# Causal attention in a two-layer decoder: keys turned one group after the queries, a new order of the prologue, and the output weights split inside the first groups

## The reference, cut to what matters

```python
qkv = jnp.einsum('bsd,de->bse', x, Wqkv)                 # 512 x 1536
q, k, v = jnp.split(qkv, 3, axis=-1)
q = _layernorm_scale_only(q, q_ln_scale)                 # over all 512 columns
k = _layernorm_scale_only(k, k_ln_scale)
scores = jnp.einsum('bshd,bthd->bhst', q / jnp.sqrt(32), k)   # 16 heads of 32
scores = jnp.where(causal, NEG_INF, scores)
attn = jax.nn.softmax(scores, axis=-1)
ctx = jnp.einsum('bhst,bthd->bshd', attn, v)
out = jnp.einsum('bsd,de->bse', ctx.reshape(B, S, D_MODEL), out_W)
```

## Time and profile before

| | |
|---|---|
| time, median of 3 runs | 2142.49 us (2141.91 to 2142.78) |
| profiled execution, its time | 2137.15 us |
| its span, first to last instruction | 2135.3 us |
| PE busy in the span | 1864.2 us (87%) |
| DVE, ACT, POOL busy | 1249.0, 920.2, 288.9 us |
| mean granted TensorE clock | 0.946 of 2.4 GHz |

### The profile page before, as it was taken

The page is one execution under the profiler, slowest core; times in us unless marked ns, Lnnn a source line. Parts: engine busy times, 40 slices in busy tenths (PEclk is TensorE's granted clock), DMA queues, the critical chain, the costliest instruction groups (busy, mean ns, idle before and its releaser), DMA issues. The chain is left out here.

```text
span 2135.3 us, 33023 instructions
## 1 busy us (share of the span) xinstructions
PE 1864.2 (87%) x12272; PEld 1514.4 (71%) x12272; DVE 1249.0 (58%) x2330; ACT 920.2 (43%) x2376; POOL 288.9 (14%) x347
## 2 busy tenths in 40 slices
PE   6979999999966899999999967888887488889966
PEld 5869999998954788888888855666665355555543
DVE  3445444444425665654565335677776378878847
ACT  2234333333323433333332224555556388888821
POOL 0000000000001111211111001223333221111001
PEclk9989999999988899999999988899998799999988
DMA  3122000000122221111110121000001377465234
GB/s 101 51 89 70 21 21 21 21 21 21 35 60 79 84 65 40 45 35 31 40 40 16 40 80 40 11 31 31 31 20 41 112 194 173 125 159 138 80 112 138
DMA packets 86253, 136.62 MB, mean 64 GB/s; under 512 B 9480, under 2 KB 25480, under 8 KB 86096
## 3 DMA queue, kind: packets, MB, share of 16 engines
q1 hardware_dynamic: 86096, 134.52, 21.8%
HBM read 79.88 MB, written 21.05 MB: 47 GB/s over the span
## 5 line engine op out<-in xcount | busy, mean ns | idle before, releaser
L1941 ACT ACTIVATE e_p<-e_s_ps,e_nb 128x512 f32<-128x512 f32 x256 | 174.8, 696 | 50.7 <-DVE e_nb L1989 49.2
L1164 PE MATMUL yp<-ccy,toep 128*128 128x288 f32 x640 | 178.7, 429 | 19.7 <-POOL ccy L892 13.6
L1433 ACT ACTIVATE p<-p,nb,rq 128x128 f32<-128x128 f32 (+1 forms) x256 | 136.8, 540 | 121.0 <-DVE nb L1524 121.0
L1989 DVE TENSOR_REDUCE e_nb<-e_s_ps 128x2 f32<-128x1024 f32 x128 | 155.7, 1217 | 50.9 <-PE e_s_ps L2066 50.9
L2076 PE MATMUL e_t_ps<-ident,e_p 128*128 128x128 f32 x1024 | 145.8, 281 | 23.8 <-DVE e_pT L1996 12.8
L1164 PEld LDWEIGHTS yp<-ccy,toep 128*128 128x128 f32 x640 | 124.0, 202 | 54.5 <-POOL ccy L892 14.8
L2076 PEld LDWEIGHTS e_t_ps<-ident,e_p 128*128 128x128 f32 x1024 | 117.9, 144 | 60.3 <-issue 50.3
L80 PE MATMUL q_ps<-a_xt_hi,wq_hi 128*128 128x256 f32 x512 | 151.9, 297 | 4.1 <-DVE wo_lo L112 4.1
L1062 DVE SCALAR_TENSOR_TENSOR hm<-gu_ps,us_col,sg 128x256 f32<-128x256 f32 x88 | 42.3, 481 | 182.0 <-ACT sg L971 182.0
L82 PE MATMUL q_ps<-a_xt_hi,wq_lo 128*128 128x256 f32 x512 | 146.6, 286 | 0.0
L81 PE MATMUL q_ps<-a_xt_lo,wq_hi 128*128 128x256 f32 x512 | 146.5, 286 | 0.0
(11 more groups left out here) (277 smaller groups left out, 5167.5 us busy)
## 6 DMA issues: line engine op xcount, KB each, us to landing
x_after<-n_r SPq DMA_DIRECT2D x24, 512.0 KB, 3.0
toep<-padded_kernels SPq DMA_DIRECT2D x32, 256.0 KB, 3.4
qs<-e_xh SPq DMA_DIRECT2D x64, 128.0 KB, 2.6
qs<-e_xl SPq DMA_DIRECT2D x64, 128.0 KB, 2.6
ks<-e_ch SPq DMA_DIRECT2D x64, 128.0 KB, 2.6
ks<-e_cl SPq DMA_DIRECT2D x64, 128.0 KB, 2.6
x<-x_after SPq DMA_DIRECT2D x12, 512.0 KB, 4.6
x<-in_x SPq DMA_DIRECT2D x8, 512.0 KB, 4.0
```

The lines of the kernel that those rows point to most:

```text
L1164: last = pe.matmul(yp[:, lo % 2, 0:NCOL], toep[h % 2][:, (lo - li) * P:(lo - li + 1) * P], ccy[h % 2][:, li, 0:NCOL], start=(li == 0), sto ...
L1433: act.activation(p[n % 3][:, h, part[t]], p[n % 3][:, h, part[t]], ACT.Exp, bias=nb[i][:, t, h:h + 1], scale=rq[u][:, t:t + 1], accum_out= ...
L1941: act.activation(pr[i][:, a, :], s_ps[i][:, a, :], ACT.Exp, bias=nb[i][:, a:a + 1], accum_out=sums[t][:, j, q:q + 1]).then_inc(e_done, 1)
L1989: dve.tensor_reduce(nb[i][:], s_ps[i][:], AX.X, ALU.max, negate=True).then_inc(nb_done, 1)
```

## The change

The computation and the number of instructions of each kind stay as they are. Four things move.

In the steps, turn_k and turned_k of tile t of the next batch go from g = t + 1 to g = t + 2, so keys of tile 0 are turned at g = 2 and those of tile 1 at g = 3; turn_q, turned_q and ACT's keys stay at g = t + 1. For batch 0 alone the units run q0, q1, k0, k1, v0, v1, with tile t in bank t (unit_bank, unit_place and unit_count keep the counts right), and queries and keys are turned into spare banks 0 and 1 by tile. In the prologue the pieces of Wq are split ahead of x, the six pieces of Wq, Wk and Wv alone are split there, and x of batch 1 is turned ahead of the value units. The two pieces of out_W are split at the end of steps 1 and 2.

```diff
-        q_bank, k_bank = spare[2], spare[3]
+        q_bank = lambda b, t: spare[2 if b else t]
+        k_bank = lambda b, t: spare[3 if b else t]
...
-        def unit_count(b, t):
+        def unit_count(b, i, t):
-            return t + 1 if b == 0 else 4 + t if b == 1 else 4 * b + t - 1
+            return i + 1 if b == 0 else 4 + t if b == 1 else 4 * b + t - 1
+        def unit_bank(b, i, t):
+            return t if b == 0 or i == 2 else i
+        def unit_place(b, i, t):
+            return 6 * b + (T * i + t if b == 0 or i == 2 else 2 * t + i)
...
# POOL, rstds
-                    pool.wait_ge(mv_done, 2 * n + 2)
+                    pool.wait_ge(mv_done, 2 * n + 2 if b else 3 + t)
...
# ACT, prologue
+                split.round_hi(act, 0, 2)
                 for r in range(2):
                     round_x(0, r)
-                split.round_hi(act, 0, len(split.pieces))
+                split.round_hi(act, 2, 6)
+                for t in range(T):
+                    turned_q(0, t)
+                for r in range(2):
+                    round_x(1, r)
                 for t in range(T):
                     keys(0, t)
-                    turned_q(0, t)
                 for t in range(T):
                     values(0, t)
-                for r in range(2):
-                    round_x(1, r)
# ACT, end of a step
+                    if n in (1, 2):
+                        split.round_hi(act, 5 + n, 6 + n)
...
# DVE, prologue
+                split.take_lo(dve, 0, 2)
                 for r in range(2):
                     lo_x(0, r)
-                split.take_lo(dve, 0, 4)
+                split.take_lo(dve, 2, 4)
                 dve.wait_ge(rows_loaded, 32)
-                for i in range(2):
-                    centre(0, 0, i)
-                split.take_lo(dve, 4, len(split.pieces))
-                for i in range(2):
-                    centre(0, 1, i)
+                for t in range(T):
+                    centre(0, t, 0)
+                split.take_lo(dve, 4, 6)
+                for t in range(T):
+                    centre(0, t, 1)
+                for r in range(2):
+                    lo_x(1, r)
                 dve.wait_ge(set_up, 3)
                 for t in range(T):
                     turned_k(0, t)
-                for r in range(2):
-                    lo_x(1, r)
# DVE, in a step and at its end
-                    if g in (1, 2) and b + 1 < B:
-                        turned_k(b + 1, g - 1)
+                    if g in (2, 3) and b + 1 < B:
+                        turned_k(b + 1, g - 2)
+                    if n in (1, 2):
+                        split.take_lo(dve, 5 + n, 6 + n)
...
# PE, prologue
-                for unit in range(6):
-                    pe.wait_ge(split.lo_done, (2, 4, 4, 4, 6, 6)[unit])
+                for unit in range(4):
+                    if unit % 2 == 0:
+                        pe.wait_ge(split.lo_done, unit + 2)
                     project(0, unit)
                 for t in range(T):
                     turn_q(0, t)
-                    turn_k(0, t)
                 for r in range(2):
                     turn_x(1, r)
+                pe.wait_ge(split.lo_done, 6)
+                for unit in (4, 5):
+                    project(0, unit)
+                for t in range(T):
+                    turn_k(0, t)
# PE, in a step
                     if g in (1, 2) and b + 1 < B:
                         turn_q(b + 1, g - 1, n + 1)
-                        turn_k(b + 1, g - 1, n + 1)
+                    if g in (2, 3) and b + 1 < B:
+                        turn_k(b + 1, g - 2, n + 1)
```

More of the change, by code:

```diff
@@ L1415, in keys @@
                     act.wait_ge(rstd_done, n + 1)
-                    act.wait_ge(p_free[1], unit_count(b, t))
+                    act.wait_ge(p_free[unit_bank(b, 1, t)], unit_count(b, 1, t))
                     act.activation(kn[t][:], kn[t][:], ACT.Copy, scale=rstd[:, t, 1:2]).then_inc(kn_done, 1)
@@ L1420, in turned_q @@
                     act.wait_ge(q_turned, T * b + t + 1)
-                    act.activation(qT[b % 2][:, :, t, :], q_bank, ACT.Copy).then_inc(q_copied, 1)
+                    act.activation(qT[b % 2][:, :, t, :], q_bank(b, t), ACT.Copy).then_inc(q_copied, 1)
                 def values(b, t):
@@ L1492, in centre @@
                     n, out, row = T * b + t, (qn, kn)[i][t], (qs_row, ks_row)[i]
-                    dve.wait_ge(p_mm, 6 * b + 2 * t + i + 1)
-                    dve.bn_stats(st[:, t, i, :], p_ps[i][:]).then_inc(st_done, 1)
+                    place, bank = unit_place(b, i, t), unit_bank(b, i, t)
+                    centred = 4 * b + place - 6 * b
+                    dve.wait_ge(p_mm, place + 1)
+                    dve.bn_stats(st[:, t, i, :], p_ps[bank][:]).then_inc(st_done, 1)
                     if b:
                         dve.wait_ge(ve_done, n - 1)
-                    dve.wait_ge(st_done, 2 * n + i + 1)
+                    dve.wait_ge(st_done, centred + 1)
                     dve.bn_aggr(mv[:, t, i, :], st[:, t, i, :]).then_inc(mv_done, 1)
-                    dve.wait_ge(mv_done, 2 * n + i + 1)
+                    dve.wait_ge(mv_done, centred + 1)
                     if b:
                         dve.wait_ge((q_turned, k_turned)[i], n - 1)
-                    dve.scalar_tensor_tensor(out[:], p_ps[i][:], mv[:, t, i, 0:1], row[:], ALU.subtract, ALU.mult)\
-                       .then_inc(p_free[i], 1)
+                    dve.scalar_tensor_tensor(out[:], p_ps[bank][:], mv[:, t, i, 0:1], row[:], ALU.subtract, ALU.mult)\
+                       .then_inc(p_free[bank], 1)
                 def turned_k(b, t):
                     dve.wait_ge(k_turned, T * b + t + 1)
-                    dve.tensor_copy(kT[b % 2][:, :, t, :], k_bank).then_inc(k_copied, 1)
+                    dve.tensor_copy(kT[b % 2][:, :, t, :], k_bank(b, t)).then_inc(k_copied, 1)
                 def masked_scores(n):
@@ L1636, in project @@
                     u = b % 2
-                    i, t = (unit % 2, unit // 2) if unit < 4 else (2, unit - 4)
+                    i, t = (unit // 2, unit % 2) if b == 0 else (unit % 2, unit // 2) if unit < 4 else (2, unit - 4)
                     p_bank(unit % 2)
@@ L1657, in turn_q @@
                 def turn_q(b, t, n=0):
-                    in_spare(2, n, q_copied, T * b + t + 1)
-                    pe.wait_ge(p_free[0], unit_count(b, t))
+                    in_spare(2 if b else t, n, q_copied, T * b + t + 1)
+                    pe.wait_ge(p_free[unit_bank(b, 0, t)], unit_count(b, 0, t))
                     for g in range(NG):
-                        last = pe.transpose(q_bank[:, g, :], qn[t][:, g * P:(g + 1) * P], core.ident[:])
+                        last = pe.transpose(q_bank(b, t)[:, g, :], qn[t][:, g * P:(g + 1) * P], core.ident[:])
                     last.then_inc(q_turned, 1)
                 def turn_k(b, t, n=0):
-                    in_spare(3, n, k_copied, T * b + t + 1)
+                    in_spare(3 if b else t, n, k_copied, T * b + t + 1)
                     pe.wait_ge(kn_done, T * b + t + 1)
                     for g in range(NG):
-                        last = pe.transpose(k_bank[:, g, :], kn[t][:, g * P:(g + 1) * P], core.ident[:])
+                        last = pe.transpose(k_bank(b, t)[:, g, :], kn[t][:, g * P:(g + 1) * P], core.ident[:])
                     last.then_inc(k_turned, 1)
```

## The result

The changed kernel takes 2087.86 us (median of 4 runs, 2083.66 to 2093.43) against 2142.2 of the kernel before (4 runs); the ratio is 0.9752, 95% interval 0.9726 to 0.9778. That is 54.3 us less where 59.0 were forecast (2083.5 us). The profiled execution took 2083.66 us with a span of 2081.9.

The account below looks back on a forecast made before the run. The prediction took PE's 14 waits for the turned keys (41.3 us) and the slow clock behind them, then the prologue, as the bound. Gains of 11.2 (prologue), 0.3 (batch 0) and 47.5 (six batches), 59.0 us, gave 2083.5, range 2073 to 2098.

Parts of the forecast that it names:

- The walk: Batch 3, g1: the values product would wait about 1.5 us for ACT's second copy of turned probabilities; g2 about 0.5.
- A batch, 40.0 forecast: Middle batch of the loop: g0 to g3 at 9.36, 11.1, 10.0 and 9.6 us sum to 40.0, against 47.9.
- The clock: Loop: 3.4 us a batch of slow clock would go, eight matmuls in each of two groups at 0.231, not 0.436.
- Rival (a): Loop: the clock still falls once a batch after g1's 1.5 us wait, costing 1.8 a batch; 2094 us, chance 0.12.
- The rule on transposes: Loop, g2 and g3: a counter-argument that 20 transposes in a row beside a short wait could bring 1.2 GHz back.
- The cover of the keys' last copy: End of g3: DVE's copy of tile 1's turned keys would finish 1.1 us before the next batch's scores need it.
- Rival (b): Loop: the wait moves to the turned keys' last copy, over 1.1 us late, costing 12 us; 2096 us, chance 0.07.
- the three signs: Wrong if a batch exceeds 41.5 us, a g0's scores wait for kT, or first scores come after 1293.
- The prologue, 11.2 forecast: Prologue: first scores at 1289.5, not 1300.69, so 11.2 us earlier, with bounds of 8 to 13.
- the slow stretch at the start: Prologue's first projections: 14 matmuls at 1.2 GHz, 6.1 us, would stay; 2 us gained if the clock rises sooner.
- Batch 0, 0.3 forecast: Batch 0: out_W's split in steps 1 and 2 takes the keys' gain; 11.4 + 13.4 = 24.8 us against 25.05.
- The bound for batch 0 without out_W: Batch 0: had out_W no cost there, it would gain some 7 us.

Follow-up runs that it names:

- e6: Changed kernel with ACT's copies of turned probabilities and queries ahead of the next batch's keys and values; 2085.99 us, ratio 0.9715 to the kernel before.
- e8: Changed kernel with ACT's copy of turned queries ahead of the next batch's values in g2; 2082.09 us in one run.
- e3: Kernel before with ten unused matmuls ahead of each of PE's 14 waits for the keys; 2125.24 us, ratio 0.9893.
- e10: Kernel before profiled again without an edit; its causal attention took 365.1 us, against 368.4 in its first profile.
- e1: Kernel before with only the keys turned one group later, prologue and out_W's split as they were; 2094.3 us, ratio 0.9756.
- e5: Changed kernel with out_W's two pieces split in the prologue where ACT and DVE idle, not in steps 1 and 2; 2083.15 us, ratio 0.9704.
- e2: Changed kernel with the keys turned in their old group, so new prologue and out_W's split alone; 2134.52 us, ratio 0.9949 to the kernel before.

## Why the prediction was right

**The stall and what takes its place.** Both parts came as walked: 3.27 and 2.85 us of waiting went, the values product waits 1.43 and 0.28. The walk said that the second copy on ACT sets it. It does in the changed kernel, but e6 shows DVE's copy of turned probabilities ending with it. The timeline of the kernel before had it already:

```profile
1458.10 0.68 DVE L1537 COPY pT<-s_ps 128x512 f32<-128x512 f32 x1
```

DVE's copy ends at 1458.78, ACT's at 1458.80. The step looked at one of two copies that the product waits for. It did not change the sum, and it misled e6.

**A batch, 40.0 forecast, 40.5 measured.** g1 lasts 11.2 us between scores (11.1 forecast), g2 10.3 (10.0), g3 9.6 (9.6), g0 9.4 (9.36). The missing 0.3 in g2 is a wait that the step for g2 left out: scores need all four banks, and the copy of the queries from bank 2 stands on ACT behind the values of the next batch. e8 gives 0.33 of it back.

**The clock.** The sum had 3.4 us a batch for it (its own terms, twice eight matmuls at 0.205 more, give 3.3); e3 measures 3.2. Rival (a), that a wait of 1.5 us would bring 1.2 GHz back, did not come: 1.00 in every middle batch. It was nearer than its text says. That the clock fell after 2.85 and 3.27 and never after 0.33 holds for batch 3. In batch 1 of the same trace a wait of 1.95 us is followed by seven slow matmuls, while in e10 the same wait is followed by none:

```profile
1362.99 0.78 PE L1668 MATMUL s_ps<-ident,kn 128*128 128x128 f32 x4 [1.95 <-ACT kn L1417]
```

So that waits of 1.4 us stayed free was not settled by the rows that the prediction read. The rule on transposes, in the Trainium skill, page TensorE: Matmul & The Clock Gate, section Part 4: PE-mode transpose, says that transposes do not bring the full clock about as matmuls do. In this trace g2 and g3 have 20 in a row among projections, at a clock of 1.00, so it costs nothing here. Only in g3 of batch 0 do they stand without projections around them: there the clock was 0.50 behind a stall of 4.95 us in the changed kernel, and 1.00 behind one of 1.28 us in e1, so the transposes alone did not bring it down either.

**The cover of the keys' last copy.** In batch 3 it ends at 1450.63, the scores start at 1451.64: 1.0 us of cover, where 1.1 was forecast.

```profile
1449.95 0.68 DVE L1522 COPY kT<-s_ps 128x512 f32<-128x512 f32 x1
...
1332.29 0.94 PE L1701 MATMUL s_ps<-kT,qT 32*128 32x128 f32 x16 [0.90 <-DVE kT L1522]
```

Rival (b) did occur once, at the end of batch 0, where the output projection does not fill g3: the scores of batch 1's g0 wait 0.90 us for kT (the second row). That is one of the three signs that the prediction had named for being wrong. The walk was made for a middle batch, where it holds; for the last step of batch 0 it had not been made.

**The prologue, 11.2 forecast.** 38.2 to 26.7, 11.5 in the first profile, 12.3 in the second (25.9). Its parts show as said: the first projection starts 3.5 us after x is turned (it was 6.0), no unit waits for a bank, and 1.33 us remain for the last copy (1.1 forecast). The term that moved is the slow stretch at the start: 14 matmuls at 1.2 GHz were carried over, 11 ran so in the first profile and 7 in the second. At 0.205 us each that is 0.6 and 1.4 us less than carried over, enough for the excess of 0.3 and 1.1 over the forecast and for the 0.8 between the two. The terms listed in the forecast add up to 9.8; the other 1.4 stood there as small gaps, and no run takes them apart.

**Batch 0, 0.3 forecast, 1.8 measured.** The two steps with out_W in them came at 11.41 and 13.34 us, to the tenth as walked (11.4 and 13.4), and are 0.3 us shorter than before, as said. The rest is in the steps around them, 8.05 and 8.70 us in place of 9.42 and 8.84. In the first profile of the kernel before, eight matmuls of the first step ran at 1.2 GHz, in the changed kernel none. In e10 none did either, and there the second step took 14.54 in place of 13.30: the first two steps together are 22.7 and 22.6 in the two profiles, 19.5 in the changed kernel. The walk measured its gain against one of the two ways in which the clock can fall there. The bound for batch 0 without out_W, 7, was too low: it is 8.7 (e1).

**The total.** The attention took 59.2 us less in the profile, by 59.0 in the sum. Part of the agreement is luck: batches 2 to 6 gained 7.3 to 7.5 each where 7.9 was said, and the 2.5 that they miss are made up by batches 0 and 1. Batch 1 gained 8.9 against the first profile of before and 5.8 against the second, so against e10 the attention gained 55.8 to 56.9. The span of the profiled execution fell by 53.4: to the 59.2 come 1.1 between the attention's last batch and the cross attention, and off go 1.6 of a later start, 5.0 of a longer cross attention and 0.3 behind it. The medians differ by 54.3 us in the first set of runs and 61.1 in the second; the 59.0 lie between. The cross attention scatters from 352 to 362 us and the start of this block from 1261.2 to 1267.9 in twelve profiles; the range had no term for either. That they also make the difference between the two sets of medians is likely and not shown, since only one execution of each set has a profile.

## What to carry to other kernels

When a step of a chain is moved one round later, walk the next round by the same rows and list every condition of the instruction that then waits: two producers that end together look like one in a trace, and only moving both frees it. In the loop here a stall of some 3 us on PE mostly cost half as much again in the slow stretch behind it, so it was worth filling even where the idle time itself could not be used. Read that price over several batches and two profiles: the same stall did not always bring it. Work that is needed once goes where both of its engines idle; at the end of a step, behind another engine's longest list, 2.4 us of DVE's work cost 6 to 7 us of batch 0 (e1, e5).

## What the runs showed of the hardware

Ten matmuls of no use in each of 14 stalls made the kernel 21.5 us faster (e3). In the middle batches of the kernel before, stalls of 2.85 to 3.27 us were each followed by six to eight projection matmuls at 0.43 us in place of 0.23, and in e3, with the stalls filled, by none; single stalls of 1.4 us in g1 of the changed kernel's middle batches were followed by none. The length of a stall does not decide alone. The clock stayed at 1.00 behind 3.27 us in two batches of e2 and behind 2.74 us in batch 0 of the kernel before; it fell behind 1.95 us in batch 1 of one profile of that kernel and not in the other; of two kernels with nearly the same three waits (1.28, 2.11 and 0.61 or 0.97 us) it fell in e5 and not in e1. What decides is open. In batch 0 of the changed kernel the granted clock was 0.50 for 3 us behind a stall of 4.95 us, and the eight transposes there took 1.97 us in place of 1.04:

```profile
1326.40 1.97 PE L1715 MATMUL s_ps<-ident,p 128*128 128x128 f32 x8 [4.95 <-DVE p L1528]
...
1326.40:1329.40 3.00, 3.00 (x14) 3.00 (x15) 2.93 (x6) 2.04 (x9) 1.90 (x1) 0.50 0.00 0
```

The cross attention, unchanged, took 352.2 to 353.5 us in the three profiles with a granted clock of 0.95 there and 356.5 to 361.7 in the nine with 0.92 to 0.94, with the work of DVE and ACT the same within about 1%.
